# Layer 0 attention of a two-layer transformer kernel: the reciprocal of the softmax sums moves from VectorE to GpSimd, as a power of minus one

## What is computed

```python
scores = jnp.einsum('bqhd,bkhd->bhqk', qf, kf) * scale
scores = jnp.where(mask[None, None], scores, jnp.finfo(scores.dtype).min)
p = jax.nn.softmax(scores, axis=-1)
o = jnp.einsum('bhqk,bkhd->bqhd', p, v)
o = o.reshape(B, T, H * D_V) @ Wo
```

## Time and profile before

| | |
|---|---|
| median of 3 runs | 574.58 us (574.08 to 575.18) |
| the profiled execution | 579.15 us, of which the span from first to last instruction is 577.3 us |
| busy over the span | PE 496.6 us (86%), DVE 399.9 (69%), ACT 337.2 (58%), POOL 301.9 (52%) |
| mean granted TensorE clock | 0.949 of full speed |
| layer 0's attention | about 40 to 186 us of the span |

### The profile page before, as it was taken

One profiled execution on the slowest core, in us unless ns is written; L12 is line 12 of the kernel. 1 busy time (PEld: TensorE's weight loads), 2 busy tenths in 40 slices (PEclk: granted clock), 3 DMA queues, 4 the chain that ended last, 5 costly groups with the idle time before them and its releaser, 6 DMA issues. The chain is left out here.

```text
span 577.3 us, 10671 instructions
## 1 busy us (share of the span) xinstructions
PE 496.6 (86%) x3418; PEld 430.0 (74%) x3434; DVE 399.9 (69%) x882; ACT 337.2 (58%) x736; POOL 301.9 (52%) x286
## 2 busy tenths in 40 slices
PE   5988999999986994399971789999999999789983
PEld 5677888888875883277750557899999999679983
DVE  2669888888871265545546666898888988485766
ACT  5537767777765345133330267888888888744413
POOL 4735777677662035545550164767767776380200
PEclk9989999999998996599995799999999999989998
DMA  8929999800000922244534000000000001300002
GB/s 275 383 57 396 314 330 327 289 0 0 0 1 10 388 78 74 74 129 140 158 108 147 1 1 1 1 1 2 0 0 0 0 0 39 107 19 1 1 2 73
DMA packets 17572, 56.67 MB, mean 98 GB/s; under 512 B 2580, under 2 KB 12314, under 8 KB 15738
## 3 DMA queue, kind: packets, MB, share of 16 engines
q1 hardware_dynamic: 14784, 49.81, 25.4%
q0 software_dynamic: 2752, 6.40, 3.3%
HBM read 49.19 MB, written 28.45 MB: 134 GB/s over the span
## 5 line engine op out<-in xcount | busy, mean ns | idle before, releaser
L989 ACT ACTIVATE probs<-bank,neg_max,q_scale 128x256 f32<-128x256 f32 (+1 forms) x128 | 63.7, 506 | 39.6 <-DVE neg_max L1330 39.6
L1593 POOL TENSOR_TENSOR probs<-probs,inv_sum 128x512 f32<-128x512 f32 x64 | 51.6, 827 | 43.9 <-DVE inv_sum L1338 43.9
L411 PE MATMUL bank<-xT_hi,w_hi 128*128 128x256 f32 (+1 forms) x144 | 46.2, 321 | 6.4 <-DVE keysT L1564 3.0
L1603 POOL TENSOR_TENSOR probs<-probs,tables 128x256 f32<-128x256 f32 x32 | 27.7, 866 | 44.8 <-ACT probs L1022 44.8
L1685 POOL DMA_INDIRECT y_rows<-y_slot,dest x31 | 30.0, 968 | 33.1 <-DVE y_slot L1541 23.5
L1585 POOL TENSOR_TENSOR swapped<-swapped,tables 128x512 f32<-128x512 f32 x32 | 42.4, 1324 | 8.8 <-ACT swapped L974 8.7
L1293 DVE TENSOR_TENSOR swapped<-bank,tables 32x512 f32<-32x512 f32 x64 | 44.4, 693 | 1.4
L1581 POOL TENSOR_TENSOR qT<-qT,swapped 128x512 f32<-128x512 f32 x32 | 40.9, 1279 | 7.8 <-DVE swapped L1293 7.8
L413 PE MATMUL bank<-xT_hi,w_lo 128*128 128x256 f32 (+1 forms) x144 | 43.2, 300 | 0.0
L412 PE MATMUL bank<-xT_lo,w_hi 128*128 128x256 f32 (+1 forms) x144 | 43.2, 300 | 0.0
L540 PE MATMUL bank<-keysT,qT 128*128 128x256 f32 x128 | 38.4, 381 | 0.7 <-ACT wo_full L1096 0.7
(11 more groups left out here) (263 smaller groups left out, 1790.9 us busy)
## 6 DMA issues: line engine op xcount, KB each, us to landing
slots<-in_c_unused SPq DMA_DIRECT2D x20, 1036.0 KB, 34.4
gu_all<-in_gate_up SPq DMA_DIRECT2D x4, 1024.0 KB, 8.9
xg<-slots SPq DMA_DIRECT2D x31, 129.5 KB, 2.1
wvo_raw<-in_wvo SPq DMA_DIRECT2D x1, 2560.0 KB, 19.6
dn_all<-in_down SPq DMA_DIRECT2D x1, 2048.0 KB, 9.0
wq_full<-in_Wq SPq DMA_DIRECT2D x1, 2048.0 KB, 15.2
yg<-y_rows SPq DMA_DIRECT2D x4, 512.0 KB, 5.1
wo_raw<-in_Wo SPq DMA_DIRECT2D x1, 2048.0 KB, 8.2
```

Source lines behind the costliest of these rows:

```text
L411: eng.matmul(dst, s_hi, m_hi, start=start, stop=False, skip_group_check=True)
L989: ins = act.activation(probs[:, par, h, c0:c1], bank[:, 2 * par + h, c0:c1], ACT.Exp, bias=neg_max[:, par, i:i + 1], scale=q_scale[:, b, t ...
L1593: ins = pool.tensor_tensor(some, some, inv, ALU.mult)
```

## The change

`row_sum` is turned into `inv_sum` by GpSimd, at the head of its normalisation, as `row_sum` to the power of a constant -1 (four columns, 128x4, both inputs in SBUF). GpSimd waits for `exp_done` and then for its own result. The reciprocal and its wait leave VectorE's body. A constant tile `minus4` is set once, behind the memset of `swapped`. The count that the two waits on `cleared` want is raised to suit.

```diff
@@ build
+    minus4 = sb("minus4", [P, 4])
@@ dve_attention0
             if own and ahead(p, b, more):
                 dve_cos(dve, at, *ahead(p, b, more))
-            if own:
-                dve.wait_ge(at["exp_done"], n + 1)
-                dve.reciprocal(inv_sum[:, par, :], row_sum[:, par, :]).then_inc(at["inv_ready"], 1)
@@ pool_normalise
+        pool.wait_ge(at["exp_done"], n + 1)
+        pool.tensor_tensor(inv_sum[:, par, :], row_sum[:, par, :], minus4[:], ALU.pow).then_inc(at["inv_ready"], 1)
         pool.wait_ge(at["inv_ready"], n + 1)
@@ gpsimd, ahead of the loop
         pool.memset(swapped[0:64], 0.0).then_inc(ld["cleared"], 1)
-        pool.wait_ge(ld["cleared"], 3)
+        pool.memset(minus4[:], -1.0).then_inc(ld["cleared"], 1)
+        pool.wait_ge(ld["cleared"], 4)
```

## The result

The changed kernel takes 585.73 us (median of 4 runs, 585.51 to 586.51), the kernel before, run beside it, 574.43 us (4 runs): ratio 1.0185, 95% interval 1.0167 to 1.0202, +11.3 us. On another chip, with more runs, it was 586.37 against 577.70 us: ratio 1.0136 (1.0109 to 1.0162), +8.7 us. There the kernel before varies from 575.0 to 580.0 us, and on a third chip from 573.8 to 580.3, so a few microseconds are a matter of the execution. Forecast was +1.7 us, with the right sign and too small by a factor of five and more; the time lies within the range.

A forecast was written before the change was run, and what follows sets the result against it. TensorE, at 17.36 us per pair, was taken as the bound, with `neg_max` held by GpSimd. The terms +0.47 + 0.20 + 0.50 - 0.03 + 0.55 = +1.69 us on 574.58 gave 576.3 us, range 572.8 to 594.

The forecast's parts named there:

- What bounds the kernel: Pair of heads: TensorE needs 17.36 of 17.54 us; `neg_max` waiting for GpSimd closes a 4.03 us loop.
- The length of the power: New GpSimd instruction, 32 times: D = 0.58 us, the middle between 0.19 and 0.98.
- What the loop becomes: Steps of a pair: one of 3.93 us, two of 4.50, one at b = 0 of 4.71, in sum 17.64.
- the fast step: Step in which `neg_max` goes through after the first of two normalising instructions: 3.35 + D, forecast 3.93 us.
- The sum for D = 0.98: Whole kernel if the power took 0.98 us: +0.56 on each of six pairs, about +6, 580.6 us.
- The sum over the kernel: Along the normalisations at b = 0: +0.47 + 0.20 + 0.50 - 0.03 + 0.55 = +1.69 us.
- the slow rival: Steps: GpSimd sets the pace and TensorE idles, with clock 0.50 behind the last steps; some 590 us, chance 0.22.
- GpSimd as the bound: Steps: from D = 1.0 nothing hides the power, each 0.1 us costs 3.1 us; chance 0.22.
- The windows that fall well: Steps: with D near 0.45 the 5.35 us step disappears, pair 17.36, -0.9 to -1.3 us; chance 0.07.
- The cheap power that changes nothing: Whole kernel: with D = 0.19 the start shifts 0.08 us and time stays 574.6 us; chance 0.16.
- The first call: First power on GpSimd: about 6 us more for code not yet loaded, 582 us; chance 1 in 20.
- Who stands behind the new waits: Behind GpSimd's two waits: normalisation, addition, `w_lo`; only the transposes feel it, the addition has over 8 us of cover.

The follow-up runs named there:

- The idle work: Changed kernel plus 64 idle multiplications on TensorE into the free query bank, in the last three steps and behind them: 584.49 us, ratio 1.0137.

## Why the prediction was right in sign and wrong in size

*What bounds the kernel.* Right. TensorE's 17.36 us per pair is the floor, and `neg_max` stands until GpSimd's instruction ends: the kernel with the maxima in PSUM shows both.

*The length of the power.* This is the step that failed. The prediction took D = 0.58, the middle between 0.19 and 0.98; it is 1.02, just above the upper end. The lower end is right for a product (0.20 us measured) and says nothing of a power, whose price per column is higher by two orders. That the indirect DMA's 0.98 came so near is luck: a power of 8 columns takes 1.81 us. That a power is a series in software was an assumption; the runs show a price for each column and not how it is made. The wait of GpSimd on itself was 0.08, taken as 0.10.

*What the loop becomes.* The two formulas, 3.35 + D for the fast step and 4.13 + D at b = 0, were right. With 0.20 the fast step is 3.55, measured 3.54, and a miss above 5.3 follows, measured 5.33; with the power twice it is 5.35, measured 5.32. At b = 0 it is 4.13 + 1.02 = 5.15, measured 5.13. The fast step at D = 1.02 (4.37, measured 4.35) tests nothing, since TensorE's own 4.34 is as long: with the maxima in PSUM the three other steps of the changed kernel still take 4.32 in the mean. What holds the pair is the step at b = 0. The sum for D = 0.98 was +0.56 per pair and some +6 in all; the steps and the first shift gave 5.0 + 0.9 (from 0.29 to 1.19 us between the first exponentials and the first normalisation).

*The sum over the kernel.* A term was missing, and its size is open. Behind the last steps there is a half-clock stretch of 10.2 us in both profiles of the changed kernel, against 3.4, none and 6.8 in three with the loop of before. Beside the profile with none, that is 1.3 us ahead of the projection (5.96 against 4.62) and 2.2 in it (9.47 against 7.31); beside the one with 6.8 it is 0.9 in all. The idle work takes the stretch away in the profile, but the times didn't fall with it. The earlier trace rows had shown that the clock falls there; the prediction used it for the slow rival alone. Against the profile with none the account is: steps 5.0, first shift 0.9, last step 1.3, projection 2.2, and 2.5 us before and behind, which vary between two profiles of before by as much. The first four make 9.4 us; beside the profiles with 3.4 and 6.8 us at half clock they would make 8.1 and 6.8. All three lie within the interval of the +8.7. Why the first chip gave +11.3 isn't settled.

*The rivals.* GpSimd as the bound was said to decide from D = 1.0: D is just there, and it decides in the one step of a pair that also holds `w_lo`, not in all. Its price beyond, 3.1 us for each 0.1 us, was too high: 24 us for a second power of 1.0 us, since two in four steps change over to GpSimd's own length. The range it gave for D = 1.5 to 2.0 (590 to above 605) fits the 610.4 us measured at 2.0. The windows that fall well didn't come; even the product was slower, though a D near 0.45 was not tried. The cheap power that changes nothing was wrong too: at 0.20 us the time rose by 3.1 us (interval 1.3 to 5.4), where the prediction had -1.5 to +2. The first call cost 0.02 us in the loop and 0.5 at the start of the kernel. The Trainium skill gives about 6 us for the first call of code that is freshly loaded (GPSIMD Engine Reference, Instruction dispatch). No first power here shows such a time, and the runs don't show whether its code had to be loaded.

*Who stands behind the new waits.* The transposes, as said: their weight loads wait in every step, 5.4 us in 20 steps, and their multiplications once per pair. In the last steps, which make no queries, the multiplications of the transposes wait too, 0.8 us in each. That `w_lo` makes the queries wait as well wasn't foreseen.

## What to carry to other kernels

An instruction of four columns can be the longest in a step: price it by the operation and the engine. Where no row has that operation, no neighbour prices it: the middle of two others was off by 0.44 us here, and the dearer one was near only for four columns. A run with that instruction alone, in an idle stretch, gives the price. Where two engines exclude each other at SBUF, look for short instructions with two SBUF inputs on the path; moving one input to PSUM took waits of up to 1.1 us out of the steps, which was worth some 1 us of 577 since TensorE was near its floor. Where two loops of nearly the same length hold a step, take each away by itself, and look at the longest step of the period first. And where a step's change lets TensorE idle, read the granted clock of what comes behind it, not only of the step.

## What the runs showed of the hardware

- A power on GpSimd takes 0.73, 1.01, 1.81 and 2.89 us for 1, 4, 8 and 16 columns on 128 partitions, a product of 4 columns 0.20.
- A VectorE instruction that stands behind a GpSimd one gets in between two GpSimd instructions though these follow each other without a gap (it ends at 128.49, the first of them at 128.47). One that is under way holds GpSimd's next back: with 0.48 us to go the power took 1.36 in place of 1.02 us, with 0.52 to go 1.39.
- With one of its two inputs in PSUM the same VectorE instruction took 161 to 164 ns in all 32 steps. The Trainium skill says that a VectorE instruction contends with a GpSimd one in a two-port performance mode, or with two inputs in SBUF when GpSimd reads SBUF (SBUF — State Buffer, the section on the two sides of SBUF). For the two inputs these runs agree; no run here tests such a mode.
- Behind the last steps, in which TensorE waited in every step, its granted clock was 0.5, that is 1.2 GHz, for 10.2 us in both profiles of the changed kernel, for 3.4 us, not at all and 6.8 us in three with the loop of before, and for 6.8 us and not at all in two of the kernel before with the maxima in PSUM. In the one profile of each of the two kernels that had multiplications in those waits it stayed at 2.4 GHz.
